# A decoder layer on one core: deeper buffering of the last stage, and VectorE's gate products cut into eight small ones

## The reference, cut to what matters

```python
logits = hidden_states @ router_w + router_b
probs = softmax(logits); topw, topi = top_k(probs, 4)
topw = topw / sum(topw)                     # four gates for each token
out  = sum over the 4 chosen experts e of  gate[e] * (gelu(x @ w1[e] + b1[e]) @ w2[e] + b2[e])
x    = layernorm(x + out)                   # (r - mean) / sqrt(var + eps)
```

## Time and profile before

| what | value |
|---|---|
| device time, median of 3 runs | 736.38 us |
| lowest and highest | 733.62 and 743.28 us |
| the profiled execution's own time | 740.4 us |
| its span in the trace | 738.6 us |
| PE busy | 533.2 us (72%) |
| DVE, ACT, POOL busy | 432.0, 373.6, 401.8 us |
| last stage, first load issued to the end of the span | 692.6 to 738.6 us |

### The profile page before, as it was taken

One profiled execution on the slowest core, in us unless ns is written; L12 is line 12 of the kernel. 1 busy time (PEld: TensorE's weight loads), 2 busy tenths in 40 slices (PEclk: granted clock), 3 DMA queues, 4 the chain that ended last, 5 costly groups with the idle time before them and its releaser, 6 DMA issues.

```text
span 738.6 us, 16361 instructions
## 1 busy us (share of the span) xinstructions
PE 533.2 (72%) x4226; PEld 419.6 (57%) x4226; DVE 432.0 (58%) x1490; ACT 373.6 (51%) x1051; POOL 401.8 (54%) x494
## 2 busy tenths in 40 slices
PE   4786987799888887888876308766766666666894
PEld 2464756576666655666654207656656566566383
DVE  4889799568766666666662684343343343434165
ACT  4577788368655555555553105444344444535146
POOL 3776564011555555555566663555665565666491
PEclk8989899789877888888885558999999999999997
DMA  5000100112222222222237433222322222221492
GB/s 186 16 17 28 36 4 13 34 42 56 74 76 66 74 69 72 66 73 66 57 80 243 119 104 87 72 78 70 84 75 74 77 72 81 65 78 51 155 337 79
DMA packets 86496, 59.20 MB, mean 80 GB/s; under 512 B 39053, under 2 KB 76947, under 8 KB 86193
## 3 DMA queue, kind: packets, MB, share of 16 engines
q1 hardware_dynamic: 76624, 41.26, 20.5%
q0 software_dynamic: 8672, 16.87, 7.0%
q10 hardware_dynamic: 1152, 0.53, 0.2%
HBM read 32.24 MB, written 23.14 MB: 75 GB/s over the span
## 4 chain that ended last, share of the span: by engine, by line
PE 22%; issue 19%; DVE 11%; DMA 8%; POOL 7%; another core or an unknown queue 4%; SPq 4%; DVEq 2%; POOLq 1%; ACT 1%; ACTq 0%
DMA ys<-yout,xin 4%; PE bank L752 3%; PE bank L984 3%; PE bank L769 3%; SPq L394 3%; POOL ys L617 3%; PE bank L974 2%; PE bank L1019 2%; POOL xs L590 2%; DVE mx L1502 2%; DMA xin<-xs 2%; PE bank L790 2%; POOL bd L571 2%; DVE yout L1765 2%
## 5 line engine op out<-in xcount | busy, mean ns | idle before, releaser
L617 POOL DMA_INDIRECT ys<-yout,xin x143 | 148.5, 1038 | 104.2 <-DVE yout L1765 68.6
L590 POOL DMA_INDIRECT xs<-xrow,slots x128 | 127.8, 998 | 105.5 <-issue 39.7
L1281 ACT ACTIVATE hid<-bank,wcur 128x128 f32<-128x128 f32 x286 | 82.3, 383 | 50.2 <-PE bank L984 40.2
L1502 DVE TENSOR_REDUCE mx<-bank 128x4 f16<-128x308 f32 x128 | 61.2, 478 | 73.1 <-PE bank L752 30.9
L1755 DVE COPY wcur<-wall 128x642 f32 x143 | 67.9, 518 | 58.3 <-DVE yout L1765 43.6
L974 PE MATMUL bank<-xinT,wcur 128*128 128x128 f32 x572 | 80.1, 283 | 20.7 <-DVE wcur L1755 16.4
L1175 ACT ACTIVATE Ex<-bank 77x512 f32<-77x512 f32 x128 | 72.7, 587 | 29.5 <-PE bank L769 16.8
L974 PEld LDWEIGHTS bank<-xinT,wcur 128*128 128x128 f32 x572 | 70.4, 194 | 27.9 <-ACT xinT L1272 18.7
L963 PE MATMUL bank<-ident,xin 128*128 128x128 f32 x143 | 30.6, 297 | 74.5 <-DMA xin<-xs 67.7
L1765 DVE TENSOR_TENSOR yout<-bank,wcur 128x256 f32<-128x256 f32 x72 | 30.2, 420 | 88.4 <-PE bank L984 59.8
L984 PE MATMUL bank<-wcur,hid 128*128 128x128 f32 x572 | 75.7, 275 | 0.1
(11 more groups left out here) (217 smaller groups left out, 1224.8 us busy)
## 6 DMA issues: line engine op xcount, KB each, us to landing
xin<-xs SPq DMA_DIRECT2D x143, 64.5 KB
yin<-ys SPq DMA_DIRECT2D x16, 512.0 KB, 10.5
qs<-qtrip SPq DMA_DIRECT2D x96, 32.0 KB
ys<-yout,xin POOLq DMA_INDIRECT x143
xTg<-xT_dram SPq DMA_DIRECT2D x8, 256.0 KB, 3.0
X<-x_dram SPq DMA_DIRECT2D x1, 2048.0 KB, 9.9
x1s<-X SPq DMA_DIRECT2D x32, 64.0 KB
qtrip<-qhl SPq DMA_DIRECT2D x32, 64.0 KB
```

The source lines that it names most:

```text
L590: pool.indirect_dma_start(words, bass.IndirectOffsetOnAxis(ap=slots[p][:, r:r + 1], axis=0), xrow[p][:, r, 0:RW], None).then_inc(s(f"scatt ...
L617: pool.indirect_dma_start(ys, bass.IndirectOffsetOnAxis(ap=xin[d][:, j, E:RW].bitcast(U32), axis=0), yout[d % WR][:, j, :], None, bounds_c ...
L1281: ins = act.activation(hid[d % 2][:, j, c, :], psH[d % 2][:, (j * NI + c) * P:(j * NI + c + 1) * P], ACT.Gelu, bias=wcur[d % WR][:, j, 2 * ...
L1502: dve.tensor_reduce(mx16[p % 2][:, j, 1:1 + QD], psL1[:, 0:QD * C].rearrange("p (h c) -> p h c", c=C), AX.X, ALU.max).then_inc(s("mx_ready ...
```

## The change

It does five things, all in the last stage:

- 16 buffers `yin` in the place of 12, so that each chunk has its own. Load f waits, from f = 8 on, until load f - 8 has landed, and no longer for a sum; eight semaphores serve the loads.
- 8 buffers each of `r3`, `o3`, `mv3`, `rs3` and `nm3` in the place of 4. The waits for them to come free reach back 8 chunks.
- 6 banks for the sums in the place of 4.
- DVE's products for chunks 4, 8 and 12 are eight `tensor_scalar` each, of 128 numbers per partition, with one gate per partition as the scalar. The product of chunk 0 stays one `tensor_tensor`.
- The chunks that each engine weighs, and the places of the products in the programs, stay as they are.

```diff
-        YB = 12
+        YB, OB = NF, 8
+        SB = 6
-        r3 = [sb(f"r3{p}", [P, FB, E]) for p in range(4)]
-        o3 = [sb(f"o3{p}", [P, FB, E]) for p in range(4)]
+        r3 = [sb(f"r3{p}", [P, FB, E]) for p in range(OB)]
+        o3 = [sb(f"o3{p}", [P, FB, E]) for p in range(OB)]
...
             def load_y(f):
-                if f >= YB:
-                    sp.wait_ge(s("sum_ps"), f - YB + 1)
-                sp.dma_start(yin[f % YB][:, :, :], y4[:, FB * f:FB * f + FB, :]).then_inc(s(f"y_in{f % YB}"), 16)
+                if f >= OB:
+                    sp.wait_ge(s(f"y_in{f % OB}"), 16)
+                sp.dma_start(yin[f % YB][:, :, :], y4[:, FB * f:FB * f + FB, :]).then_inc(s(f"y_in{f % OB}"), 16)
...
-                free(pe, "r3_ready", f - 3)
+                free(pe, "r3_ready", f - SB + 1)
                 for j in range(TOP):
-                    mm = pe.matmul(banks[f % 4][:, 0:FB * E].rearrange("p (c e) -> p c e", c=FB), ident[:, :], yin[f % YB][:, :, j * E:(j + 1) * E],
+                    mm = pe.matmul(banks[f % SB][:, 0:FB * E].rearrange("p (c e) -> p c e", c=FB), ident[:, :], yin[f % YB][:, :, j * E:(j + 1) * E],
...
-                if f >= 4:
-                    act.wait_ge(s(f"out{f % 4}"), 16 * (f // 4))
+                if f >= OB:
+                    act.wait_ge(s(f"out{f % OB}"), 16 * (f // OB))
...
-                free(dve, "x3_ready", f - 3)
+                free(dve, "x3_ready", f - OB + 1)
...
+            def weigh(f):
+                dve.wait_ge(s(f"y_in{f % OB}"), 16 * (f // OB) + 16)
+                for c in range(FB):
+                    for j in range(TOP):
+                        y = yin[f][:, c, j * E:(j + 1) * E]
+                        ins = dve.tensor_scalar(y, y, gates[:, FB * f + c, j:j + 1], None, ALU.mult)
+                ins.then_inc(s("weighed_by_dve"), 1)
 
             weigh_rows(dve, 0).then_inc(s("weighed_by_dve"), 1)
             for f in range(NF + 2):
                 if f + 2 in BY_DVE:
-                    weigh_rows(dve, f + 2).then_inc(s("weighed_by_dve"), 1)
+                    weigh(f + 2)
                 if f < NF:
                     gather(f)
```

More of the change, by code:

```diff
@@ L190, in build @@
         NF = B // FB
-        YB = 12
+        YB, OB = NF, 8
         BY_DVE, BY_ACT = [f for f in range(NF) if f % 4 == 0], [1]
+        SB = 6
         BY_POOL = [f for f in range(NF) if f not in BY_DVE and f not in BY_ACT]
-        r3 = [sb(f"r3{p}", [P, FB, E]) for p in range(4)]
-        o3 = [sb(f"o3{p}", [P, FB, E]) for p in range(4)]
+        r3 = [sb(f"r3{p}", [P, FB, E]) for p in range(OB)]
+        o3 = [sb(f"o3{p}", [P, FB, E]) for p in range(OB)]
         st3 = [sb(f"st3{p}", [P, FB, 6]) for p in range(2)]
-        mv3 = [sb(f"mv3{p}", [P, FB, 2]) for p in range(4)]
+        mv3 = [sb(f"mv3{p}", [P, FB, 2]) for p in range(OB)]
         ln3 = [sb(f"ln3{p}", [P, FB]) for p in range(2)]
-        rs3, nm3 = ([sb(f"{n}{p}", [P, FB]) for p in range(4)] for n in ("rs3", "nm3"))
+        rs3, nm3 = ([sb(f"{n}{p}", [P, FB]) for p in range(OB)] for n in ("rs3", "nm3"))
         second_part = ExitStack()
@@ L268, in weigh_rows @@
             share = gates[:, FB * f:FB * f + FB, :].unsqueeze(3).to_broadcast([P, FB, TOP, E])
-            eng.wait_ge(s(f"y_in{f % YB}"), 16 * (f // YB) + 16)
+            eng.wait_ge(s(f"y_in{f % OB}"), 16 * (f // OB) + 16)
             return eng.tensor_tensor(y4, y4, share, ALU.mult)
@@ L414, in load_y @@
             def load_y(f):
-                if f >= YB:
-                    sp.wait_ge(s("sum_ps"), f - YB + 1)
-                sp.dma_start(yin[f % YB][:, :, :], y4[:, FB * f:FB * f + FB, :]).then_inc(s(f"y_in{f % YB}"), 16)
+                if f >= OB:
+                    sp.wait_ge(s(f"y_in{f % OB}"), 16)
+                sp.dma_start(yin[f % YB][:, :, :], y4[:, FB * f:FB * f + FB, :]).then_inc(s(f"y_in{f % OB}"), 16)
             def store(f):
                 sp.wait_ge(s("x3_ready"), f + 1)
-                sp.dma_start(out[:, FB * f:FB * f + FB, :], o3[f % 4][:, :, :]).then_inc(s(f"out{f % 4}"), 16)
+                sp.dma_start(out[:, FB * f:FB * f + FB, :], o3[f % OB][:, :, :]).then_inc(s(f"out{f % OB}"), 16)
             for f in range(NF):
@@ L427, in _ @@
                 store(f)
-            for p in range(4):
-                sp.wait_ge(s(f"out{p}"), 16 * (NF // 4))
+            for p in range(OB):
+                sp.wait_ge(s(f"out{p}"), 16 * (NF // OB))
         @block.gpsimd
@@ L1305, in scales3 @@
                 free(act, "rs3_ready", f - 1)
-                act.activation(ln3[f % 2][:, :], mv3[f % 4][:, :, 1], ACT.Ln, bias=EPS).then_inc(s("ln3_ready"), 1)
+                act.activation(ln3[f % 2][:, :], mv3[f % OB][:, :, 1], ACT.Ln, bias=EPS).then_inc(s("ln3_ready"), 1)
                 act.wait_ge(s("ln3_ready"), f + 1)
-                act.activation(rs3[f % 4][:, :], ln3[f % 2][:, :], ACT.Exp, scale=-0.5).then_inc(s("rs3_ready"), 1)
+                act.activation(rs3[f % OB][:, :], ln3[f % 2][:, :], ACT.Exp, scale=-0.5).then_inc(s("rs3_ready"), 1)
             def normal3(f):
                 act.wait_ge(s("nm3_ready"), f + 1)
-                if f >= 4:
-                    act.wait_ge(s(f"out{f % 4}"), 16 * (f // 4))
+                if f >= OB:
+                    act.wait_ge(s(f"out{f % OB}"), 16 * (f // OB))
                 for c in range(FB):
-                    ins = act.activation(o3[f % 4][:, c, :], r3[f % 4][:, c, :], ACT.Identity, scale=rs3[f % 4][:, c:c + 1], bias=nm3[f % 4][:, c:c + 1])
+                    ins = act.activation(o3[f % OB][:, c, :], r3[f % OB][:, c, :], ACT.Identity, scale=rs3[f % OB][:, c:c + 1], bias=nm3[f % OB][:, c:c + 1])
                 ins.then_inc(s("x3_ready"), 1)
             def weigh(f):
-                act.wait_ge(s(f"y_in{f % YB}"), 16 * (f // YB) + 16)
+                act.wait_ge(s(f"y_in{f % OB}"), 16 * (f // OB) + 16)
                 for c in range(FB):
@@ L1789, in gather @@
                 dve.wait_ge(s("sum_ps"), f + 1)
-                free(dve, "x3_ready", f - 3)
-                dve.tensor_tensor(r3[f % 4][:, :, :], banks[f % 4][:, 0:FB * E].rearrange("p (c e) -> p c e", c=FB), X[:, FB * f:FB * f + FB, :], ALU.add).then_inc(s("r3_ready"), 1)
+                free(dve, "x3_ready", f - OB + 1)
+                dve.tensor_tensor(r3[f % OB][:, :, :], banks[f % SB][:, 0:FB * E].rearrange("p (c e) -> p c e", c=FB), X[:, FB * f:FB * f + FB, :], ALU.add).then_inc(s("r3_ready"), 1)
             def stats(f):
@@ L1795, in stats @@
                 for c in range(FB):
-                    ins = dve.bn_stats(st3[f % 2][:, c, :], r3[f % 4][:, c, :])
+                    ins = dve.bn_stats(st3[f % 2][:, c, :], r3[f % OB][:, c, :])
                 ins.then_inc(s("st3_ready"), 1)
@@ L1802, in spread @@
                 for c in range(FB):
-                    ins = dve.bn_aggr(mv3[f % 4][:, c, :], st3[f % 2][:, c, :])
+                    ins = dve.bn_aggr(mv3[f % OB][:, c, :], st3[f % 2][:, c, :])
                 ins.then_inc(s("mv3_ready"), 1)
@@ L1808, in shift3 @@
                 for c in range(FB):
-                    ins = dve.tensor_scalar(nm3[f % 4][:, c:c + 1], mv3[f % 4][:, c, 0:1], rs3[f % 4][:, c:c + 1], -1.0, ALU.mult, ALU.mult)
+                    ins = dve.tensor_scalar(nm3[f % OB][:, c:c + 1], mv3[f % OB][:, c, 0:1], rs3[f % OB][:, c:c + 1], -1.0, ALU.mult, ALU.mult)
                 ins.then_inc(s("nm3_ready"), 1)
+            def weigh(f):
[5 more added lines that the diff above has]
+                ins.then_inc(s("weighed_by_dve"), 1)
             weigh_rows(dve, 0).then_inc(s("weighed_by_dve"), 1)
```

## The result

| | median | ratio to the kernel before |
|---|---|---|
| before | 738.01 us | |
| changed | 747.69 us (4 runs, 744.25 to 750.89) | 1.013, 95% interval 1.009 to 1.017 |

The change costs 9.7 us by the medians (four runs each). The profiled execution of the changed kernel took 744.25 us with a span of 742.3; its first load of the last stage was issued at 686.95, that is 5.7 us earlier than in the profiled execution of before, which is scatter of stages that the change doesn't touch. So the last stage is compared by its own landmarks, and not by the spans. From the first `gather` to the last it is 40.3 us (695.76 to 736.09) where it was 31.4. The tail behind the last gather is 6.2 us in both.

What follows compares the result with a forecast made beforehand. PE was taken to set the last stage's pace; chunk 4's turns with POOL delay it to 715.6, then 20.8 + 1.9 us put the last gather at 738.3, 5.9 us later: 736.4 + 5.9 = 742.3 us, range 730 to 749.

Steps and rivals of the forecast that it cites:

- rival 2: Chunk 4 on DVE: POOL already in chunk 5, all eight small products wait; 745.2 us, ceiling 749; chance 0.16.
- PE sets the pace, and its waits of 5.4 us are all there is to win: Last stage: PE needs 1.73 us per chunk; its waits, 5.4 us, are the most the deeper buffers can save.
- Loads at no cost: Last stage's loads: each now waits for the one eight earlier, with seven still queued, so costed at nothing.
- The two engines exclude each other, and the small products contend with POOL: DVE and POOL products: each excludes the other for one whole instruction, small ones too; 1.87 us per POOL product.
- L1471's 0.45 us beside 0.23: Earlier 128 x 128 row with one scalar per partition, beside POOL: 0.22 us extra, read as contention, open to two readings.
- Turns of one instruction each: DVE and POOL alternate one instruction each, so each waiting small product costs a whole POOL product, 1.92 us with the turn.
- The rows near 70 us: Earlier trace records of DVE and POOL starting alternately, six in a row, taken as showing turns.
- Two slip through, six wait: 11.9 us: Chunk 4 on DVE, 703.61 to 715.5: two small products precede POOL's chunk 5, six wait 1.92 us each; PE idles 9.5 us.
- The clock's 1.9 us: PE after its long idle: low granted clock at the start adds 1.9 us to twelve chunks' 20.8 us.
- Chunks 8 and 12 add nothing: DVE's later small products: POOL is done by then, eight take 1.2 us, and PE does not wait.
- Rivals 1 and 3: Small products run without turns, 731.0 us, chance 0.22; or two or more pass per turn, 741 us, chance 0.10.

Runs made afterwards that it cites:

- e1: The changed kernel with DVE's products of chunks 4, 8 and 12 as one large tensor_tensor again, deeper buffers kept; ratio 0.9955 to the kernel before.
- e7: The changed kernel with POOL waiting ahead of chunks 5, 9 and 13 until DVE's products of chunks 4, 8 and 12 are done; ratio 0.9954 to the kernel before.
- e4: The changed kernel with DVE's small products reading their tensor operand from a PSUM bank instead of SBUF (other data); ratio 0.9947 to the kernel before.
- the changed kernel again: The changed kernel, nothing altered, run once more on a later chip over 6 runs; 667.26 us, ratio 1.0150 to the kernel before.
- e3: The changed kernel with DVE's products as two, four or eight tensor_tensor pieces; ratios to the kernel before 0.9965 (two), 1.0155 (eight), none for four.
- e5: The changed kernel with the constant 0.25 in place of the gate in DVE's small products; one run, no ratio, chunk 4 in 11.45 us.
- e2: The kernel before with only the eight small products put in, old buffers kept; ratio 1.0154 to the kernel before.
- e8: Large products and deeper buffers, with chunks shared anew among DVE, ACT and POOL and one PE filler less; 652.33 us, ratio 0.9916 to the kernel before.
- e6: The changed kernel with each of POOL's products cut into two of 512; ratio to the kernel before 1.0157 over four runs, 1.0089 over 11 runs.

## Why the prediction was right, and which term was too small

The prediction was 742.3 us and slower by 5.9; measured were 747.7 and 9.7. Sign and mechanism held, and the size was short by almost 4 us. In the trace the step is 8.9 us, 3.0 more than forecast: PE's wait was 12.24 us where the sum has 9.5, and the low clock cost 0.2 us more than its term. The 0.8 us between 8.9 and 9.7 is within what four runs leave open. The measured time is 5.4 us above the forecast, and it lies in the stated range because rival 2 (745.2 to 749 us) is in it.

- *PE sets the pace, and its waits of 5.4 us are all there is to win.* Held: e1 and e7 take them away, and gather to gather falls by 5.0 and 5.1 us.
- *Loads at no cost.* Held. In e1 they are issued over 13.6 us as before, and no engine waits for the landing of one behind chunk 5.
- *The two engines exclude each other, and the small products contend with POOL.* Held (e7, e4). By the records DVE's large product ends 1.1 us behind POOL's (713.22 to 712.14), not 1.2. L1471's 0.45 us beside 0.23 was a sign of it, but the scalar operand has a part too: alone, the form with the gate takes 0.28 us and the constant 0.22.
- *Turns of one instruction each.* Held, in all eight records of chunk 4. The rows near 70 us were enough to read it from.
- *Two slip through, six wait: 11.9 us.* This is the mis-sized term. In the profiled execution POOL's chunk 5 began at 698.14, DVE's products at 698.35, and all eight waited: 14.74 us. I took the order of one trace, where POOL was 0.23 us later. Rival 2 was written for this case, "It decides from a shift of 0.23 us of a landing", with 8.8 us for the last gather; measured were 8.9. Its chance of 0.16 was too low: a margin of 0.23 us on a landing is close to even. In the ten traces with POOL's whole products and no hold on them, DVE's chunk 4 began ahead of POOL's chunk 5 in five (before, the changed kernel again, e1, e3 in two, e5, by 0.02 to 0.23 us) and behind it in five. Of the three profiled executions with eight small `tensor_scalar` by the gate and POOL's whole products, two had POOL first (the changed kernel and e2), and one (the changed kernel again) DVE, with 11.57 us and a PE wait of 9.1 where the forecast had 11.9 and 9.5.
- *The clock's 1.9 us.* Held in the profiled execution: twelve chunks took 22.90 us, 2.1 more than 12 x 1.73, and the granted clock was 0.51 over the first 4 us. But it was too small for the very case that the forecast describes. In the two executions where PE waited 9.1 and 9.0 us (the changed kernel again and e5), twelve chunks took 23.67 and 23.52 us, 2.9 and 2.8 more, and the granted clock of the second 4 us was 0.81 and 0.84, where it was 1.00 after the wait of 12.24 us. Why the shorter wait costs more isn't settled. The changed kernel again, to be read with the stretches above:

```profile
638.70:642.70 4.00, 4.00 (x16) 3.39 (x15) 2.56 (x17) 1.98 (x7) 1.48 (x1) 0.81 0.19 64
```

- *Chunks 8 and 12 add nothing.* Held in time, though eight take 1.65 us by themselves and not 1.2; I had put the two of them 0.13 us apart, and they are 0.19.
- *Rivals 1 and 3* fell: in no trace do the small products run in groups between POOL's. The one near thing is e5's second product, which starts 0.03 us after the record of POOL's first and still goes through.

## What to carry to other kernels

Before cutting a VectorE instruction like these (float32, `tensor_scalar` or `tensor_tensor` with all tensors in SBUF) into small ones, look at what GpSimd does at that time: if it has long products like these queued, from SBUF to SBUF, count the pieces and multiply by the length of *its* instruction, not of yours. In chunk 4, beside whole products of GpSimd's, one large instruction paid that at most once, and eight paid it six to eight times. A PSUM source (e4) and an idle GpSimd (e7) paid it not at all, nor did ScalarE: its eight products took 2.44 us in e1 and in e8, where 0.8 and 1.4 us of them lay beside a product of GpSimd's. Where such a meeting hangs on a transfer that lands within some tenths of a microsecond, price both orders.

## What the runs showed that I had not expected

- To let DVE in costs POOL next to nothing when DVE's instruction is small: nine products in 16.73 us with eight `tensor_scalar` of 128 between them, 1.86 each, as without. It grows with the length of DVE's instruction: in e3 one of POOL's products took 1.94, 2.07 and 2.34 us with a piece of 128, 256 and 512 in front of it, and 2.87 behind a whole one of 1024, for 1.89 by itself.
- The scalar from SBUF has a price of its own: eight small products beside an idle POOL take 1.65 us with the gate and 1.16 with a constant (e5, chunk 8). From PSUM they take 2.15.
- The other stages scatter about as much as the whole effect: in the profiled executions the last stage began at 678 to 687 us on one chip (e1, e2, e6, e7) and at 690 to 695 on another (e3 in two and eight, e4, e5). Its length from gather to gather, in kernels without a meeting of small products, was 26.3 and 26.4 us in three executions (e1, e4, e7).
